# Third edge phase of a graph network: gathering rows of x W1x + b1 in place of rows of x, with host-transposed edge attributes

## The reference, cut to what matters

```
hidden[e] = relu(concat(x[src[e]], edge_attr_32[e]) @ W1 + b1)     # 96 -> 128 columns
          = relu((x @ W1x + b1)[src[e]] + edge_attr_32[e] @ W1e)   # the same, W1x: 64 rows, W1e: 32 rows
mean[n]   = segment_mean(hidden, dst)                              # then W2, b2 and the update layers
```

## Time and profile before

| What | Value |
|---|---|
| time, median of 3 runs | 8994.63 us |
| span of the profiled execution | 12212.0 us |
| POOL busy in the profiled span | 6789.5 us (56%) |
| DVE, ACT, PE busy | 4710.0, 3336.3, 2780.2 us |
| DMA, mean over the span | 80 GB/s |

### The profile page before, as it was taken

The page is one execution under the profiler, slowest core; times in us unless marked ns, Lnnn a source line. Parts: engine busy times, 40 slices in busy tenths (PEclk is TensorE's granted clock), DMA queues, the critical chain, the costliest instruction groups (busy, mean ns, idle before and its releaser), DMA issues. The chain is left out here.

```text
span 12212.0 us, 65741 instructions
## 1 busy us (share of the span) xinstructions
PE 2780.2 (23%) x15715; PEld 2525.3 (21%) x15715; DVE 4710.0 (39%) x6608; ACT 3336.3 (27%) x4637; POOL 6789.5 (56%) x6997
## 2 busy tenths in 40 slices
PE   2000000011000000044444444444333332333333
PEld 1000000010000000034334333333232222322233
DVE  3455555555666666432222222222231111111113
ACT  0222222233222222132222222222242232232231
POOL 6666666657777777644444444444435544544543
PEclk6555555555555555577666667667655555555556
DMA  6232323312222222222222222222111211211121
GB/s 270 91 99 95 98 95 99 99 47 74 98 98 94 98 93 96 69 75 76 76 76 76 76 76 76 75 73 79 39 42 55 63 62 55 63 62 59 59 62 52
DMA packets 366486, 982.75 MB, mean 80 GB/s; under 512 B 163828, under 2 KB 173582, under 8 KB 351652
## 3 DMA queue, kind: packets, MB, share of 16 engines
q1 hardware_dynamic: 135572, 667.06, 14.4%
q0 software_dynamic: 224608, 290.88, 9.4%
q10 hardware_dynamic: 6192, 23.73, 0.5%
HBM read 582.50 MB, written 398.69 MB: 80 GB/s over the span
## 5 line engine op out<-in xcount | busy, mean ns | idle before, releaser
L771 POOL DMA_INDIRECT se<-x_table,edge_ix x1512 | 1428.3, 945 | 1867.2 <-PEq L1343 1397.1
L771 POOL DMA_INDIRECT comb<-x_table,edge_ix x1512 | 1428.8, 945 | 1468.3 <-DMA edge_ix<-in_src 1010.4
L771 POOL DMA_INDIRECT g<-x_table,edge_ix x1512 | 1585.4, 1049 | 512.2 <-issue 512.2
L771 POOL DMA_INDIRECT qv<-qv_table,edge_ix x1484 | 1406.5, 948 | 681.1 <-issue 445.6
L889 DVE TENSOR_TENSOR_SCAN edge_val<-edge_bank,edge_val 128x464 f32<-128x464 f32 (+1 forms) x715 | 687.4, 1031 | 2469.3 <-ACT edge_val L1597 2462.9
L1565 PE MATMUL h_ps<-w_hidden,edge_comb_t 97*128 97x128 f32 x3136 | 699.3, 394 | 1924.3 <-issue 964.5
L899 ACT ACTIVATE edge_sums<-edge_val 128x1904 f32<-128x1904 f32 (+3 forms) x219 | 1107.0, 5055 | 0.0
L1454 DVE TENSOR_TENSOR edge_product<-mk_ps,edge_q_now 128x256 f32<-128x256 f32 x392 | 166.4, 424 | 2364.2 <-ACT edge_msg L1393 2344.8
L1565 PEld LDWEIGHTS h_ps<-w_hidden,edge_comb_t 97*128 97x128 f32 x3136 | 613.2, 291 | 2000.2 <-ACT edge_comb_t L1592 1009.0
L1353 PE MATMUL mk_ps<-w_mk,edge_se_t 128*128 128x128 f32 x3136 | 545.9, 329 | 1659.7 <-issue 1412.0
L1353 PEld LDWEIGHTS mk_ps<-w_mk,edge_se_t 128*128 128x128 f32 x3136 | 483.1, 235 | 1709.1 <-issue 1424.3
(11 more groups left out here) (416 smaller groups left out, 9145.2 us busy)
## 6 DMA issues: line engine op xcount, KB each, us to landing
sums<-edge_sums SPq DMA_DIRECT2D x56, 1848.0 KB
sums<-edge_sums SPq DMA_DIRECT2D x55, 1792.0 KB, 6.6
sums<-edge_sums SPq DMA_DIRECT2D x56, 1008.0 KB
sums<-edge_sums SPq DMA_DIRECT2D x55, 924.0 KB, 3.7
edge_k<-k_edges SPq DMA_DIRECT2D x56, 896.0 KB
edge_bond<-in_edge_attr SPq DMA_DIRECT2D x56, 896.0 KB
edge_eh<-in_edge_attr SPq DMA_DIRECT2D x56, 896.0 KB
edge_qr<-in_edge_attr_n SPq DMA_DIRECT2D x56, 896.0 KB
```

What stands on the lines that cost most here:

```text
L771: e.indirect_dma_start(self.gather_into(u, j), None, self.gather_from, bass.IndirectOffsetOnAxis(ap=now[:, j:j + 1], axis=0))\
```

## The change

- **Node phase 2** makes x @ W1x + b1 for every group, also for the last three: PE multiplies the turned x by `w3_x` (64 rows twice on the diagonal, 256 columns for a pair of nodes) beside `w3_ux`, DVE adds b1 (`take_hidden`, lag 20), and SP stores 128 columns into `hidden_table`. x itself is no longer stored. The attributes' weights `w3_e` (four times on the diagonal, 128 x 512) are loaded by 8 DMAs at its start.
- **Edge phase 3** gathers rows of 128 columns of `hidden_table` straight into `g`. The host hands in the attributes transposed, so that a chunk is 128 x 896 and PE can use it as it comes: 7 multiplications of 512 columns each by `w3_e` into seven PSUM banks. DVE adds them to `g` in two pieces, of 16 and 12 columns (`add`), ACT does the relu and turns the piece into `val` (`light`), and the scans and the layout stay. Transposes, `move` and the copy of the attributes are gone.
- The last chunk's layout of its first 20 columns moves behind the second add on DVE; the layout of the last but one chunk goes from DVE (L1653) to ACT.

```
--- before.py
+++ after.py
@@ edge_phase_3
+        g = [ctx.enter_context(nc.sbuf_tensor(f"hidden{b}", [P, J, P], F32)) for b in (0, 1)]
+        ph = EdgePhase(p, 3, ctx, p.hidden_table, lambda b, j: g[b][:, j, :], quads)
+        ea_t = [ph.sb(f"ea_t{b}", [P, quads, P]) for b in (0, 1)]
+        halves = (slice(0, 4 * QUAD), slice(4 * QUAD, J))
...
         @block.tensor
             with e.Fori(0, ph.rounds) as i:
                 for b in (0, 1):
+                    ph.wait_attrs(e, i, b, 1)
+                    for half, of in enumerate(halves):
+                        e.wait_ge(added, at(i, 4, 2 * b + half + 1))
+                        for q in range(of.start // QUAD, of.stop // QUAD):
+                            last = e.matmul(e_banks[:, q, :], ea_t[b][:, q, :], p.w3_e, start=True, stop=True)
+                        last.then_inc(made, 1)
...
         @block.scalar
+            def light(i, b):
+                for half, of in enumerate(halves):
+                    e.wait_ge(added, at(i, 4, 2 * b + half + 3))
+                    e.activation(ph.val[b][:, :, 1 + of.start:1 + of.stop], g[b][:, of, :].rearrange("p j f -> p f j"),
+                                 ACT.Relu).then_inc(taken, 1)
+                e.drain().then_inc(ph.rows_free[b], 1)
...
         @block.vector
+            def add(i, b):
+                for half, of in enumerate(halves):
+                    for c in range(of.start // QUAD, of.stop // QUAD):
+                        ph.wait_part(e, i, b, c)
+                    e.wait_ge(made, at(i, 4, 2 * b + half + 1))
+                    if half:
+                        e.sem_inc(ph.attr_free[b], 1)
+                    e.tensor_tensor(g[b][:, of, :], g[b][:, of, :], e_ps[:, of, :], ALU.add)
+                    e.drain().then_inc(added, 1)
@@ node_phase_2
+            def multiply_next(g):
+                e.wait_ge(times_next.moved, g + 1)
+                after(e, taken, g)
+                turned = times_next.tile_t[g % 2]
+                for k in range(times_next.pairs(g)):
+                    last = e.matmul(hidden_ps[:, k, :], turned[:, k, :], p.w3_x[:, :], start=True, stop=True)
+                last.then_inc(made, 1)
                 if g < early:
...
+            def take_hidden(g):
+                n = ph.sizes[g]
+                after(e, stored[g % outs], 16 * (g // outs))
+                e.wait_ge(made, g + 1)
+                e.tensor_tensor(hidden_out[g % outs][:, 0:n, :],
+                                hidden_ps.rearrange("p k (u f) -> p (k u) f", u=2)[:, 0:n, :],
+                                bcast(p.param["L3_gnn_msg_b1"][:, :], 1, n), ALU.add)
+                e.drain().then_inc(taken, 1)
```

More of the change, by code:

```diff
@@ L715, in sync @@
             e.sem_inc(self.stored[b], 1)
-            load(b, slice(b * J, (b + 1) * J))
+            load(b, b)
         def turn(i):
@@ L1582, in _ @@
         def _(e):
[L1583 to L1619, removed]
@@ new lines, in _ @@
+            with e.Fori(0, ph.rounds - 1) as i:
+                for b in (0, 1):
+                    light(i, b)
+                    ph.lay_out(e, i, b)
+            i = ph.rounds - 1
+            light(i, 0)
+            ph.lay_out(e, i, 0)
+            for more in (0, 1):
+                now = ph.columns(more)
+                e.wait_ge(added, 4 * i + 5 + more)
+                e.activation(ph.part(more)[:, :, 1:], g[1][:, now, :].rearrange("p j f -> p f j"), ACT.Relu)\
+                    .then_inc(taken, 1)
@@ L1629, in _ @@
         def _(e):
+            e.sem_inc(added, 2)
             ph.clear_carries(e)
@@ L1646, in _ @@
                     begin(i, b)
+                    add(i, b)
                     sum_up(i, b)
@@ L1649, in _ @@
             begin(i, 0)
-            e.sem_inc(opened, 1)
+            add(i, 0)
             sum_up(i, 0)
-            e.wait_ge(ph.stored[0], 16 * i + 1)
-            e.tensor_copy(ph.sums[0][:, :, :], ph.val[0][:, :, 1:].rearrange("p f j -> p j f")).then_inc(ph.ready[0], 1)
-            e.drain().then_inc(ph.val_free[0], 1)
+            e.wait_ge(made, 4 * i + 4)
             for more in (0, 1):
@@ L1660, in _ @@
                 ph.carry_part(e, i, more)
-                if more == 0:
-                    e.sem_inc(opened, 1)
-                e.wait_ge(taken, i * per + quads + now.stop // QUAD + 2)
+                for c in range(now.start // QUAD, now.stop // QUAD):
+                    ph.wait_part(e, i, 1, c)
+                e.tensor_tensor(g[1][:, now, :], g[1][:, now, :], e_ps[:, now, :], ALU.add)
+                e.drain().then_inc(added, 1)
+                if more:
+                    ph.lay_out_cut(e, e.tensor_copy)
+                e.wait_ge(taken, 4 * i + 3 + more)
                 for part in range(8):
@@ L2250, in _ @@
         def _(e):
-            for g in range(groups):
-                ph.store(e, g, p.x_tables[2])
-            e.wait_ge(ph.out, 16 * groups)
+            e.wait_ge(w_zeroed, 1)
+            for n in range(QUAD):
+                for k in range(2):
+                    e.dma_start(p.w3_e[n * 32:(n + 1) * 32, n * P + k * FD:n * P + (k + 1) * FD],
+                                p.ins["L3_gnn_msg_w1"][k, FD:FD + 32, :]).then_inc(w_in, 16)
+            table = p.hidden_table.rearrange("(p t) f -> p t f", p=P)
+            for g in range(groups):
+                e.wait_ge(taken, g + 1)
+                e.dma_start(table[:, ph.now(g), :], hidden_out[g % outs][:, 0:ph.sizes[g], :])\
+                    .then_inc(stored[g % outs], 16)
+            e.wait_ge(w_in, 16 * 2 * QUAD)
+            for u in range(outs):
+                e.wait_ge(stored[u], 16 * len(range(u, groups, outs)))
         @block.gpsimd
@@ L2262, in turn_next @@
             def turn_next(g):
-                if g < early:
-                    times_next.turn(e, g, p.x[:, ph.now(g), :])
-            def multiply_next(g):
-                if g < early:
-                    times_next.multiply(e, g, p.w3_ux)
+                times_next.turn(e, g, p.x[:, ph.now(g), :])
+            def multiply_next(g):
[5 more added lines that the diff above has]
+                last.then_inc(made, 1)
+                if g < early:
+                    after(e, times_next.used, g)
+                    for k in range(times_next.pairs(g)):
+                        last = e.matmul(times_next.h_ps[0][:, k, :], turned[:, k, :], p.w3_ux[:, :],
+                                        start=True, stop=True)
+                    last.then_inc(times_next.done, 1)
+                else:
+                    e.drain().then_inc(times_next.done, 1)
             in_turn(groups,
@@ L2308, in _ @@
         def _(e):
+            e.memset(p.w3_e, 0.0)
+            e.drain().then_inc(w_zeroed, 1)
             times_w.clear(e)
@@ L2348, in _ @@
                     (13, lambda g: second.sum_squares(e, g)),
-                    (15, lambda g: second.turn_over(e, g)), per=4)
+                    (15, lambda g: second.turn_over(e, g)),
+                    (20, take_hidden), per=4)
 def node_phase_3(p):
```

77 lines of the change are left out of this document (36 added, 41 removed).

## The result

| | before | after | ratio, 95% |
|---|---|---|---|
| time, median of 13 runs each | 8993.04 us | 9013.35 us | 1.0024 (1.0016 to 1.0031) |
| span of the profiled execution | 12212.0 us | 9009.6 us | |
| POOL, DVE, ACT, PE busy in that span | 6789.5, 4710.0, 3336.3, 2780.2 us | 6621.4, 4952.5, 3194.3, 2350.8 us | |

The change costs 20 us (14 to 28), 0.24%: slower by little more than this kernel's measurement can tell. The forecast was 9018, +23 us.

What follows compares the result with a forecast made beforehand. POOL's indirect DMAs, issued nearly without a break, were taken to bound the kernel, with DVE setting node phase 2. Setup 0, edge phase 3 +2 and node phase 2 +21 make 8995 + 23 = 9018 us; range 8690 to 9060.

Steps and rivals of the forecast that it cites:

- POOL sets the edge phases, the quads are hidden: Edge phase 3: POOL needs 32.7 us a chunk, PE and ACT about 29, so removing the quads gains 0 us.
- 1.17 us for an indirect DMA: POOL in the timed runs: each of 6958 indirect DMAs takes 1.17 us, 7% less than in the profile.
- the 872 us: POOL's time without issue beyond the named waits: setup, ends of phases and node phases, taken as present in timed runs.
- The waits belong to the profiled execution: POOL's 2643 us of named waits, 1010 in edge phase 3, are in the profiled execution and not in timed runs.
- Rival A: Part of edge phase 3's 1010 us of waits is in the timed runs and goes: priced at 8700 us; chance 0.20.
- Prices of the added work: Edge phase 3, a chunk: DVE's adds 2.3 and 1.7 us, ACT's relu 3.7 and 2.8, PE 11, all beside POOL.
- Node phase 2, +21: DVE sets node phase 2; the added add, PE's order and last stages cost 21 us, bounds 8 and 35.
- 4 for the tail: End of node phase 2: four stages stand behind the last `finish` (turn, move, multiply, take), 4 us.
- 2 for PE's order: Node phase 2: PE's sum of 10.4 us a group against DVE's 10.0 asks 0 to 8 us more, taken as 2.
- 2 for the end of the edge phase: End of edge phase 3: DVE's add, copy and scans and ACT's relu after the last row, +2 us, -3 to +6.
- Rival B: Edge phase 3: POOL's issue slows as in edge phase 1, 104 ns x 1568 = 163 us, 9181 us; chance 0.07.
- a span near 11230 us: Whole profiled execution after the change: the 1010 us of waits go, span from 12212 to about 11230 us, time unchanged.

Runs made afterwards that it cites:

- e10: The kernel before with the changed node phase 2 alone (x stored as well, edge phase 3 of before), against before: 9012.63 us, ratio 1.0023.
- e8: The changed kernel, unchanged, run again beside the kernel before at 8992.08 us: 9012.99 us, ratio 1.0025.
- e5: The changed kernel, unchanged, against the kernel before on another chip, where before is slow: 11421.44 against 12217.11 us, ratio 0.9350.
- e9: The changed kernel with ACT copying the product in node phase 2 and DVE adding b1 in edge phase 3, against before: 8998.87 us, ratio 1.0008.

## Why the prediction was right, and where it was not

**POOL sets the edge phases, the quads are hidden: right for the timed runs.** e10's phase of before has POOL without a wait, and the change of that phase moves the total by 9012.99 - 9012.63 = +0.4 us, no more than noise. From first to last gather the phase takes 1958.0 us in e8 and 1960.1 in e10, a gain of 2.1, and the end costs 3.0 (I had +2).

**1.17 us for an indirect DMA: wrong.** It is 1.249, as in the profile. The failing term is the 872 us that I held to be work outside POOL's issue in every run. The profile after has 9009.6 - 6958 x 1.249 = 319 us in its place: the node phases and the ends are longer on the second kind too (POOL waits 142.0 us for the end of node phase 2 in e5, 59.2 in after). So more of the difference was waits, and the DMA keeps its price. A cross-check was at hand: the same chunk shows a steady 1.25 us beside idle engines, so a lower price had no row. The chunk's cover was thus 35.0 us, not 32.7, and the conclusion stood.

**"The waits belong to the profiled execution": right in what it left out of the sum, wrong in its reason.** They come with the chip. That a profile and a set of times may come from different chips I didn't weigh; I put the difference on the recording. The sum from the timed 8995 us, which leaves the waits little room, carried the forecast. Luck is in it in so far as the change was timed on the first kind again: on the second it is worth -796 us, and nothing in the prediction said which it would be.

**Rival A at 0.20: false for the comparison, true elsewhere.** On the second kind the edge phase gains 830 us. My price of 8700 was for a part of the waits inside 8995 us; none of the chips seen lies in between.

**Prices of the added work: right.** DVE's adds 2.29 and 1.75 us (2.3 and 1.7 predicted), ACT's turning relu 3.71 and 2.82 (3.7 and 2.8). The exception is PE, whose record is 0.953 us, not 0.79, so 13.3 us a chunk in place of 11, hidden with the rest.

**Node phase 2, +21: right in the sum and in what sets it, its parts nearly.** DVE's add is 1.08 us and a group's period grew by 1.22 (10.11 or 10.12 against 8.90), where I had 1.1. But the first add comes five groups behind (lag 20, a new group every 4 steps), so the first four periods stay near POOL's pace (8.7 to 9.2 us in e8). From the first group's start to the last's e8 takes 137.5 us and e9 125.4: 12 us, and not 1.22 for each of 13 groups. In time the add off DVE is worth 14.1 us (e9 against e8), where I had 14 + 1. e9 keeps 6.8 us over before, with an interval that just takes in 0; I had 4 for the tail, 2 for PE's order and 2 for the end of the edge phase, and no run parts them.

**Rival B, on the first kind: false**, the rows of 128 columns cost 944 ns as all others. The rule of the Trainium skill (GPSIMD Engine Reference, Specifications) asks for two SBUF inputs or a 2-port mode before DVE disturbs GpSimd; the first kind agrees, since the adds from PSUM stand beside gathers of 944 ns. On the second kind the two phases with such adds have 1038 and 1051 ns and the others 946 and 950, which looks like the adds' doing. But in e5 the gathers that overlap an add take 951 ns, so there too the trace agrees with the rule.

**The profile after, "a span near 11230 us": missed for the chip that it came from, near for the other.** e5's span is 11419.4. The missing 189 us is of the size of rival B's term: its gathers of `hidden` stretch over 2168.3 us, 1958.0 on the first kind, 210 us more, of which 143 us are longer gathers and the rest longer gaps between them.

**Open:** why PE's signals are late beside POOL on the second kind, and whether its work is. The changed kernel shows it too: eight records of 512 columns are signalled 17.2 us (median) after they may start in e5, 6.1 us in the profile after. In the chunk of e5 at 10129 us the other six follow 16.8 us later, so PE takes most of a chunk of 38.7 us and just fits. In what the two kinds of chip differ no run here shows.

## What to carry to other kernels

Set the profile's span against the timed median before anything else; where they are far apart, they may be of different machines, and each wait in the profile is then worth its full size or nothing. Forecast both and give the chance to the machine, not to a part of the wait. A change that takes PE's work out of a loop beside POOL's DMAs gains nothing where PE had room and much where it hadn't (+0.24% and -6.5% here, with the product's cost in both).

Work moved out of a hidden loop into a phase that one engine's order sets is paid there, 1.08 us for an add and 1.22 us in the period, once the pipeline is full. Put it on the engine with room (e9, -14 us), or back under the loop's cover.

## What the runs showed that I had not expected

One kernel takes 8992 us on some chips and 12217 to 12275 us on others, steady within 0.2% on each, with the same durations of nearly all single instructions: the difference is in when PE's signals come while POOL issues, and in POOL's own DMA in two of four phases (1038 to 1051 against 944 ns). Once POOL has issued its last DMA the two kinds are alike: a group of node phase 2 takes 10.11 us in e5 once the gathers are over, as in the profile after.
